# First expert layer: the bias of the normalisation moves from GpSimd to VectorE

## The chip, the core and the metric

The kernel runs on one core of a Trainium2 chip. The metric is the device time of one execution in microseconds, the median of three. The engines are named as the profile names them: PE (TensorE, matrix products), DVE (VectorE), ACT (ScalarE), POOL (GpSimd) and SP (the queue that issues most of the loads and stores). Each engine works through its own list of instructions in order, and a semaphore wait in that list holds everything behind it.

## What is computed

Two layers, each a recurrent or attention branch multiplied by the SiLU of a mixture of experts, over 8 sequences of 512 tokens of width 128. What matters here is in the first layer. Its branch is a state-space scan over 256 channels and 16 states, its experts are 24 two-layer experts in 4 groups with a layer norm and a ReLU between the two layers:

```
h = dA * h + dBx                       # the scan, per channel and state
h1 = moe_apply(xf, combine, dispatch, W1, b1)
h1 = (h1 - mean) / sqrt(var + eps) * lw + lb
h1 = relu(h1)
out = moe_apply(h1, combine, dispatch, W2, b2)
```

The change touches `* lw + lb`: `lw` and `lb` are the normalisation's weight and bias, one row of 512 for each of the four groups.

## The kernel before

The first layer's scan and its experts run beside each other in one block (`scan_stage`, with `Moe0Experts` as `beside`). The scan has 64 steps: for each of 8 sequences, 8 pairs of states. In a step DVE forms two products with the broadcast B row (L783) and two with the C row of the step before (L793), each 128x1024 with one operand in PSUM, and then makes two scans (L811), 128x1024 with both operands in SBUF. Some steps have more: at the step's place q within its sequence, q = 0 and 1 end with a small product (L748, L752), q = 1 has the gate (L772), and q = 3 and 6 end with the four operations of a softplus (L760 to L766). PE broadcasts the rows into three PSUM buffers (L653), sums the states (L684), and ACT makes the decays (L596).

The experts' work is laid between these steps by `side_by_side` (L469): each engine's scan generator yields at fixed places, and at each of them the experts' generator for that engine is advanced by one `yield`. So the order on an engine is written out at build time; nothing decides it at run time but the semaphores. DVE's scan generator yields twice in a step: behind the four products, and behind the two scans (and the softplus or small product that follows them).

From about step 22 the experts are in their combination. It goes over 16 units of two token tiles (128 tokens each). For one unit POOL gathers four blocks of first-layer outputs from DRAM (L1434), PE adds the gathered blocks and the experts' bias in PSUM (L1528, L1532), ACT copies the sum, takes mean and variance, refines the reciprocal root and centres the rows (L1643), POOL multiplies by `ln_w` and adds `ln_b` (L1454, L1456, each 128x1024, all operands in SBUF), ACT applies the ReLU (L1636), and SP stores the rows.

POOL's list has, for each unit u, the four gathers of unit u+1 and then the two arithmetic instructions of unit u-3 (`weigh`). These two wait for a window of the scan: `wait_window(FIRST_WINDOW + n)` with `FIRST_WINDOW = 26` lets unit n's arithmetic start when the scans of step 25+n are done, or, where that step ends with a softplus, when the softplus is done. Unit n's ReLU on ACT waits for the semaphore `weighted`, which the addition raises. The rows live in a ring of six tiles (`self.ro`), so that three units are under way.

DVE has no part in the combination before the change: `Moe0Experts.vector` sets two constants and ends.

Of the kernel before, what the change touches and what calls it, by code (L numbers as in the profile page):

```python
# [20 lines left out]
ALU = mybir.AluOpType  # L21
# [15 lines left out]
HG, E0, C0, HID = 4, 24, 86, 512  # L37
# [11 lines left out]
class Chain:  # L49


    def __init__(self, eng, sem):
        self.eng, self.sem, self.n = eng, sem, 0
# [425 lines left out]
PE_SLOTS, ACT_SLOTS, DVE_SLOTS = 4, 2, 2  # L479
# [826 lines left out]
class Moe0Experts:  # L1306
# [13 lines left out]
    def __init__(self, nc, ctx, w, r, arena, xn_dram, W1, y1_rows, r_dram, W2, y2_rows, gathered,  # L1320
                 w1_in):
        self.nc, self.w, self.r = nc, w, r
        self.xn_rows = xn_dram.rearrange("p t d -> (p t) d")
        self.y1_rows = y1_rows
        self.y1_dram = y1_rows[0:NO_ROW, :].rearrange("(h e c) n -> h e c n", h=HG, e=E0)
        self.r_dram, self.r_rows = r_dram, r_dram.rearrange("p t n -> (p t) n")
        self.W1, self.W2 = W1, W2
        self.y2_dram = y2_rows[0:NO_ROW, :].rearrange("(h e c) n -> h e c n", h=HG, e=E0)
        s = Scope(nc, ctx, "e")


        weights = Arena(arena[:, 0:3 * HID])
        self.w1 = weights.sb("w1", [P, 3, HID])
        self.w2 = self.w1.rearrange("p r (f d) -> p r f d", f=FC)
        first, middle, second = (Arena(arena[:, 3 * HID:]) for _ in range(3))
        self.xg = first.sb("xg", [CP, 4, HG, XW])
        self.xgT = first.sb("xgT", [P, 2, HG * CP])
        self.out1 = first.sb("out1", [CP, 2, HG, HID])
        self.yk = middle.sb("yk", [P, 4, 2, HID])
        self.hb = middle.sb("hb", [P, 4, HID])  # L1340
        self.ro = middle.sb("ro", [P, 6, HID])
        self.rg = second.sb("rg", [CP, 3, HG, HID])
        self.rT = second.sb("rT", [P, 3, FC * CP])
        self.out2 = second.sb("out2", [CP, 2, HG, D])
        self.stats = s.sb("stats", [P, NT, 3])
        self.total = s.sb("total", [P, NT])
        self.square = s.sb("square", [P, NT])
        self.rstd = s.sb("rstd", [P, NT])
        self.nm = s.sb("nm", [P, NT])
        self.squares = s.sb("squares", [P, HID])  # L1350
        self.eps = s.sb("eps", [P, 2])
        self.eps_set = s.sem("eps_set")
        self.newton = s.sem("newton")
        self.log_ready = s.sem("log_ready")
        self.bank = s.ps("bank", [P, 2, 512])
        self.scanned = self.u_ready = None
        self.chain = s.sem("chain")
        self.mean_ready = s.sem("mean_ready")
        self.piece_made = s.sem("piece_made")
        self.piece_read = s.sem("piece_read")  # L1360
        self.biased = s.sem("biased")
        self.combined = s.sem("combined")
        self.var_ready = s.sem("var_ready")
        self.scale_ready = s.sem("scale_ready")
        self.centred = s.sem("centred")
        self.p_chain = s.sem("p_chain")
        self.weighted = s.sem("weighted")
        self.r_ready = s.sem("r_ready")
        self.turned2 = s.sem("turned2")
        self.rT_ready = s.sem("rT_ready")  # L1370
        self.product2 = s.sem("product2")
        self.out2_ready = s.sem("out2_ready")
        self.w1_in = w1_in
        self.gathered1, self.gathered_y, self.gathered2 = gathered[0:4], gathered[4:8], gathered[8:11]
        self.stored1 = [s.sem(f"stored1{i}") for i in range(2)]
        self.stored_r = [s.sem(f"stored_r{i}") for i in range(3)]
        self.w2_in = [s.sem(f"w2_in{i}") for i in range(3)]
        self.stored2 = [s.sem(f"stored2{i}") for i in range(2)]
# [36 lines left out]
    def pool(self, pool):  # L1415
        nc, r = self.nc, self.r

        def gather_x(e):
            if e >= E0:
                return  # L1420
            if e >= 4:
                pool.wait_ge(self.piece_read, 5 * (e - 3))
            for h in range(HG):
                nc.gpsimd.indirect_dma_start(  # L1424
                    out=self.xg[:, e % 4, h, :], out_offset=None, in_=self.xn_rows,
                    in_offset=bass.IndirectOffsetOnAxis(ap=r.tab[:, h, e:e + 1], axis=0),
                ).then_inc(self.gathered1[e % 4], 16)

        def gather_y(u):
            for t in range(2 * u, min(2 * u + 2, NT)):  # L1430
                if t >= 4:
                    pool.wait_ge(self.biased, t - 3)
                for k in range(2):
                    nc.gpsimd.indirect_dma_start(  # L1434
                        out=self.yk[:, t % 4, k, :], out_offset=None, in_=self.y1_rows,
                        in_offset=bass.IndirectOffsetOnAxis(ap=r.back[:, k, t:t + 1], axis=0),
                    ).then_inc(self.gathered_y[t % 4], 16)

        def wait_window(i):

            b, q = divmod(i - 1, DS // 2)
            if q in (3, 6):
                pool.wait_ge(self.u_ready, 2 * (b + 1) + (q - 3) // 3 + 1)
            else:
                pool.wait_ge(self.scanned, 2 * i)

        def weigh(u):

            pool.wait_ge(self.centred, 2 * u + 2)
            wait_window(FIRST_WINDOW + u)  # L1450
            t = 2 * u
            ro = self.ro[:, t % 6:t % 6 + 2, :]
            g = slice(t % HG, t % HG + 2)
            nc.gpsimd.tensor_tensor(ro, ro, self.w["ln_w"][:, g, :], ALU.mult).then_inc(self.p_chain, 1)  # L1454
            pool.wait_ge(self.p_chain, u + 1)
            nc.gpsimd.tensor_tensor(ro, ro, self.w["ln_b"][:, g, :], ALU.add).then_inc(self.weighted, 1)  # L1456

        def gather_r(e):
            if e >= E0:
                return  # L1460
            if e >= 3:
                pool.wait_ge(self.turned2, HG * (e - 2))
            for h in range(HG):
                nc.gpsimd.indirect_dma_start(  # L1464
                    out=self.rg[:, e % 3, h, :], out_offset=None, in_=self.r_rows,
                    in_offset=bass.IndirectOffsetOnAxis(ap=r.tab[:, h, e:e + 1], axis=0),
                ).then_inc(self.gathered2[e % 3], 16)

        for e in range(E0):
            gather_x(e + self.AHEAD)  # L1470
            yield
        for i in range(2):
            pool.wait_ge(self.stored1[i], 16 * (E0 // 2))
        gather_y(0)
        yield
        for u in range(self.UNITS + 4):
            gather_y(u + 1)
            if 3 <= u < self.UNITS + 3:
                weigh(u - 3)
            yield  # L1480
        for i in range(3):
            pool.wait_ge(self.stored_r[i], 16 * len(range(i, self.UNITS, 3)))
        for e in range(self.AHEAD):
            gather_r(e)
        yield
        for e in range(E0):
            gather_r(e + self.AHEAD)
            yield
# [202 lines left out]
    def vector(self, dve):  # L1691
        nc, r, v = self.nc, self.r, self.nc.vector
        link = Chain(dve, self.chain)
        link(v.memset(self.eps[:, 0:1], 1e-6))
        v.memset(self.eps[:, 1:2], 1.5).then_inc(self.eps_set, 1)
        yield


class Moe0Output:
# [117 lines left out]
    def link(self, dve, ins):  # L1817
        self.linked += 1
        ins.then_inc(self.d_chain, 1)
        dve.wait_ge(self.d_chain, self.linked)  # L1820
# [1197 lines left out]
```

## Time and profile before

| | us |
|---|---|
| median of 3 runs | 1442.43 (1440.59 to 1442.75) |
| the profiled execution: its own time | 1438.98 |
| the profiled execution: its span | 1436.1 |
| DVE busy in the span | 1199.1 (83%) |
| PE busy in the span | 1258.3 (88%) |
| ACT busy in the span | 883.8 (62%) |
| POOL busy in the span | 681.2 (47%) |

The span runs from the first to the last instruction recorded; the execution's own time is 2.9 us longer. The shares are averages over stages that are limited by different engines, so the stretch in which the change lies is read by itself. That stretch is steps 26 to 40 of the scan, from 371.55 to 551.63 us of the span: from the end of step 25's scans, behind which POOL's first multiplication starts, to the start of step 41's products.

### The profile page before, as it was taken

The numbers are of one execution on the slowest core, as the hardware profiler recorded it, in microseconds if no ns is written. First come the engines' busy times: TensorE is split into PE (matmuls) and PEld (weight loads), VectorE is DVE, ScalarE is ACT, GpSimd is POOL, SyncE is SP. The second block draws the span as 40 slices with busy tenths as digits, with TensorE's granted clock in tenths as the row PEclk, the third lists the DMA queues.
The fourth block names the chain that finished last, engine by engine and source line by source line (L and its number), as shares of the span: only waits on it lengthen the run. The fifth ranks groups of instructions, "written<-read, shape, count | busy, mean of one in ns | idle before, by whom it ended". The sixth has DMA issues, their size and how long they took to land. (4 is left out here: it accounts for less than half of the span.)

```text
span 1436.1 us, 21390 instructions
## 1 busy us (share of the span) xinstructions
PE 1258.3 (88%) x7254; PEld 874.3 (61%) x7260; DVE 1199.1 (83%) x2410; ACT 883.8 (62%) x2114; POOL 681.2 (47%) x633
## 2 busy tenths in 40 slices
PE   6988798887988865999897997799999999999997
PEld 5444354443443433888896775467667777777775
DVE  6868999998888889999996778688898755568876
ACT  5577667575988885556553657756456444544462
POOL 0026565615688855655651775338640143146300
PEclk9999999999889977999998899899999999999999
DMA  8014555455233422445552721010002044213200
GB/s 257 1 24 114 144 144 155 130 142 150 90 107 128 133 74 84 136 138 142 163 146 61 235 53 37 15 42 4 1 2 59 7 111 127 62 33 49 28 29 31
DMA packets 86021, 128.82 MB, mean 90 GB/s; under 512 B 15488, under 2 KB 50657, under 8 KB 85306
## 3 DMA queue, kind: packets, MB, share of 16 engines
q1 hardware_dynamic: 66458, 75.70, 18.0%
q0 software_dynamic: 19456, 51.77, 14.0%
q8 instruction: 58, 0.95, 0.3%
q14 instruction: 49, 0.40, 0.1%
HBM read 86.66 MB, written 40.77 MB: 89 GB/s over the span
## 5 line engine op out<-in xcount | busy, mean ns | idle before, releaser
L811 DVE TENSOR_TENSOR_SCAN sc_st<-sc_dA,sc_st 128x1024 f32<-128x1024 f32 x128 | 291.0, 2317 | 0.0
L2359 DVE COPY at_pT<-at_p_t 128x512 f32<-128x512 f32 (+1 forms) x192 | 108.8, 599 | 105.2 <-PE at_p_t L2136 105.0
L793 DVE TENSOR_TENSOR sc_st<-sc_st,sc_p_bc 128x1024 f32<-128x1024 f32 x128 | 155.7, 1217 | 31.6 <-PE sc_p_bc L653 31.5
L596 ACT ACTIVATE sc_dA<-sc_dt,g_state 128x511 f32<-128x511 f32 x256 | 168.8, 709 | 6.2 <-DVE sc_st L811 5.5
L783 DVE TENSOR_TENSOR sc_st<-sc_u,sc_p_bc 128x1024 f32<-128x1024 f32 x128 | 155.1, 1212 | 7.5 <-PE sc_p_y L684 6.5
L1464 POOL DMA_INDIRECT g_state<-r_scratch,moe_tab x96 | 122.2, 1273 | 82.0 <-PE e_bank L1560 55.2
L1424 POOL DMA_INDIRECT g_state<-xn_scratch,moe_tab x88 | 117.5, 1335 | 84.3 <-ACT g_state L1584 48.1
L2232 ACT ACTIVATE at_pr<-at_pr,at_nmx 128x512 f32<-128x512 f32 (+3 forms) x256 | 140.2, 552 | 23.3 <-DVE at_nmx L2318 23.2
L2116 PE MATMUL at_p_s<-g_xT,at_qT 128*128 128x512 f32 (+3 forms) x512 | 149.4, 435 | 0.0
L653 PE MATMUL sc_p_bc<-sc_bc,mamba_sel 96*128 96x512 bf16 x256 | 102.4, 401 | 51.3 <-DVE sc_st L783 47.4
L684 PEld LDWEIGHTS sc_p_y<-g_ident,sc_st 128*128 128x128 f32 x1024 | 121.7, 144 | 27.5 <-issue 14.1
L684 PE MATMUL sc_p_y<-g_ident,sc_st 128*128 128x128 f32 x1024 | 136.1, 277 | 2.0 <-DVE sc_st L793 1.9
L1434 POOL DMA_INDIRECT g_state<-y_scratch,moe_back x64 | 93.1, 1455 | 56.8 <-DMA y_scratch<-g_state 32.3
L2318 DVE CUSTOM_DVE_ANT_0 at_pr<-at_p_s,l_mask_wide 128x512 f32<-128x512 f32 (+3 forms) x256 | 110.4, 486 | 6.0 <-PE at_p_s L2116 5.5
L2116 PEld LDWEIGHTS at_p_s<-g_xT,at_qT 128*128 128x128 f32 x512 | 83.0, 191 | 50.2 <-issue 32.1
L1513 PE MATMUL e_bank<-g_state 128*96 128x512 f32 x192 | 99.0, 614 | 10.7 <-ACT g_state L1574 10.6
L1547 PE MATMUL e_bank<-g_state 128*96 128x128 f32 x768 | 101.7, 276 | 4.4 <-ACT g_state L1675 4.0
L1584 ACT ACTIVATE g_state<-e_bank,g_state 96x512 f32<-96x512 f32 x96 | 65.0, 680 | 62.1 <-PE e_bank L1513 60.3
L2136 PEld LDWEIGHTS at_p_t<-g_ident,at_pr 128*128 128x128 f32 x640 | 74.8, 141 | 43.0 <-DVE at_pT L2359 31.5
L2136 PE MATMUL at_p_t<-g_ident,at_pr 128*128 128x128 f32 x640 | 91.6, 274 | 6.9 <-DVE at_pT L2359 6.0
L1684 ACT ACTIVATE g_state<-e_bank 128x384 f32<-128x384 f32 x96 | 46.8, 487 | 77.7 <-PE e_bank L1560 77.6
L2570 POOL DMA_INDIRECT f_m<-y_scratch,l_back x64 | 60.4, 943 | 71.7 <-DMA y_scratch<-f_out 33.4
(343 smaller groups left out, 2718.9 us busy)
## 6 DMA issues: line engine op xcount, KB each, us to landing
y_scratch<-g_state SPq DMA_DIRECT2D x24, 768.0 KB, 5.2
g_state<-W SPq DMA_DIRECT2D x48, 256.0 KB, 5.5
r_scratch<-g_state SPq DMA_DIRECT2D x16, 512.0 KB, 2.6
y_scratch<-g_state SPq DMA_DIRECT2D x24, 192.0 KB, 2.7
xn_scratch<-g_state SPq DMA_DIRECT2D x16, 256.0 KB, 4.2
g_state<-x SPq DMA_DIRECT2D x4, 512.0 KB, 7.0
g_state<-xn_scratch SPq DMA_DIRECT2D x8, 256.0 KB, 5.8
g_state<-x SPq DMA_DIRECT2D x1, 2048.0 KB
```

What stands on the lines that cost most here:

```text
L596: ins = nc.scalar.activation(dA[:, m % 4, j, 1:L], dt[:, b % 2, h, 1:L], ACT.Exp, scale=negA[:, h, 2 * q + j:2 * q + j + 1])
L684: ins = nc.tensor.matmul(p_y[:, t, h * P:(h + 1) * P], st[:, m + h, j, t * P:(t + 1) * P], w["ident"], is_transpose=True, start=False, sto ...
L783: nc.vector.tensor_tensor(st[:, m % RS:m % RS + 2, j, :], u[:, b % 2, :, :], p_bc[:, k % 3, :].unsqueeze(1).broadcast_to([P, HALF, L]), AL ...
L793: nc.vector.tensor_tensor(states, states, p_bc[:, k % 3, :].unsqueeze(1).broadcast_to([P, HALF, L]), ALU.mult).then_inc(row_used, 1)
L811: nc.vector.tensor_tensor_scan(st[:, m % RS, :, :].rearrange("p a b -> p (a b)"), dA[:, m % 4, :, :].rearrange("p a b -> p (a b)"), st[:, ...
L1424: nc.gpsimd.indirect_dma_start(out=self.xg[:, e % 4, h, :], out_offset=None, in_=self.xn_rows, in_offset=bass.IndirectOffsetOnAxis(ap=r.ta ...
L1464: nc.gpsimd.indirect_dma_start(out=self.rg[:, e % 3, h, :], out_offset=None, in_=self.r_rows, in_offset=bass.IndirectOffsetOnAxis(ap=r.tab ...
L2116: ins = nc.tensor.matmul(p_s[:, bank, c:c + K], qT[:, n % 3, i * P:(i + 1) * P], xaT[:, b, 0:K], start=True, stop=True)
L2136: ins = nc.tensor.transpose(p_t[:, bank, c + (i - j) * P:c + (i - j + 1) * P], pr[:, n % 3, sbank, sc + j * P:sc + (j + 1) * P], w["ident"])
L2232: ins = nc.scalar.activation(row, row, ACT.Exp, scale=-1.0, bias=nmx[:, n % 2, i:i + 1], accum_out=sums[:, n % 4, i:i + 1])
L2318: ins = v.tensor_tensor_reduce(out=pr[:, n % 3, bank, c:c + K], in0=p_s[:, bank, c:c + K], in1=w["mask_wide"][:, L - K:L], scale=1.0, scal ...
L2359: v.tensor_copy(pT[:, n % 2, part, 0:cols], p_t[:, PT_BANK[part], 0:cols]).then_inc(pT_ready, 1)
```

## The change

The addition of `ln_b` is taken from POOL and given to DVE. POOL's `weigh` keeps its two waits (for the centred rows and for the window of the scan) and its multiplication, which now raises a new semaphore, `multiplied`; the wait between multiplication and addition on POOL goes. `Moe0Experts.vector` gets a loop: it passes 50 yields (two for each of `E0 + 1` units), and then, in unit n's turn, waits for `multiplied` and adds `ln_b`, which raises `weighted`.

```
-        self.p_chain = s.sem("p_chain")
+        self.multiplied = s.sem("multiplied")
...
-            nc.gpsimd.tensor_tensor(ro, ro, self.w["ln_w"][:, g, :], ALU.mult).then_inc(self.p_chain, 1)
-            pool.wait_ge(self.p_chain, u + 1)
-            nc.gpsimd.tensor_tensor(ro, ro, self.w["ln_b"][:, g, :], ALU.add).then_inc(self.weighted, 1)
+            nc.gpsimd.tensor_tensor(ro, ro, self.w["ln_w"][:, g, :], ALU.mult).then_inc(self.multiplied, 1)
...
-        yield
+        yield from [None] * (DVE_SLOTS * (E0 + 1))
+        for u in range(self.UNITS + 4):
+            yield
+            if 3 <= u < self.UNITS + 3:
+                n = u - 3
+                ro = self.ro[:, 2 * n % 6:2 * n % 6 + 2, :]
+                dve.wait_ge(self.multiplied, n + 1)
+                v.tensor_tensor(ro, ro, self.w["ln_b"][:, 2 * n % HG:2 * n % HG + 2, :],
+                                ALU.add).then_inc(self.weighted, 1)
+            yield
```

On DVE, the list at the end of step 25 and in step 26 stands as follows before the change. `sc_st` are the states, `sc_p_bc` a broadcast row in PSUM; L811 are the scans.

```order
L811 SCALAR_TENSOR_TENSOR sc_st<-sc_dA,sc_st 128x1024 [waits sc_decay_ready,sc_row_used]
L811 SCALAR_TENSOR_TENSOR sc_st<-sc_dA,sc_st 128x1024 [waits sc_decay_ready]
L752 TENSOR_TENSOR sc_bc<-sc_logs 32x512 [waits sc_mid_copied]
L783 TENSOR_TENSOR sc_st<-sc_u,sc_p_bc 128x2x512 [waits sc_hc_used,sc_row_ready,sc_bc_done]
L793 TENSOR_TENSOR sc_st<-sc_st,sc_p_bc 128x2x512 [waits sc_scanned,sc_row_ready]
```

After it, the same place and on to the next addition. `g_state` is the ring of rows, `moe_ln_b` the bias.

```order
L811 SCALAR_TENSOR_TENSOR sc_st<-sc_dA,sc_st 128x1024 [waits sc_decay_ready,sc_row_used]
L811 SCALAR_TENSOR_TENSOR sc_st<-sc_dA,sc_st 128x1024 [waits sc_decay_ready]
L752 TENSOR_TENSOR sc_bc<-sc_logs 32x512 [waits sc_mid_copied]
L1701 TENSOR_TENSOR g_state<-g_state,moe_ln_b 128x1024 [waits e_multiplied,sc_bc_done]
L783 TENSOR_TENSOR sc_st<-sc_u,sc_p_bc 128x2x512 [waits sc_hc_used,sc_row_ready]
L793 TENSOR_TENSOR sc_st<-sc_st,sc_p_bc 128x2x512 [waits sc_scanned,sc_row_ready]
L783 TENSOR_TENSOR sc_st<-sc_u,sc_p_bc 128x2x512 [waits sc_row_ready]
L793 TENSOR_TENSOR sc_st<-sc_st,sc_p_bc 128x2x512 [waits sc_scanned,sc_row_ready]
L811 SCALAR_TENSOR_TENSOR sc_st<-sc_dA,sc_st 128x1024 [waits sc_decay_ready,sc_row_used]
L811 SCALAR_TENSOR_TENSOR sc_st<-sc_dA,sc_st 128x1024 [waits sc_decay_ready]
L1701 TENSOR_TENSOR g_state<-g_state,moe_ln_b 128x1024 [waits e_multiplied]
```

Sixteen additions (L1701) stand each between a step's scans and the next step's products, in steps 25 to 40.

On POOL, the difference at the first two units. L1434 are the gathers, L1454 the multiplications.

```order
 L1454 TENSOR_TENSOR g_state<-g_state,moe_ln_w 128x1024 [waits sc_scanned,e_centred]
-L1456 TENSOR_TENSOR g_state<-g_state,moe_ln_b 128x1024 [waits e_p_chain]
-L1434 DMA g_state<-y_scratch,moe_back 128x512 [waits e_biased]
-L1434 DMA g_state<-y_scratch,moe_back 128x512
-L1434 DMA g_state<-y_scratch,moe_back 128x512 [waits e_biased]
-L1434 DMA g_state<-y_scratch,moe_back 128x512
-L1454 TENSOR_TENSOR g_state<-g_state,moe_ln_w 128x1024 [waits sc_scanned,e_centred]
-L1456 TENSOR_TENSOR g_state<-g_state,moe_ln_b 128x1024 [waits e_p_chain]
```

The sixteen additions go from this list; gathers and multiplications keep their order, and each multiplication keeps its wait for `sc_scanned` (or `sc_u_ready`).

## Rows read from the trace of the kernel before

**Rows 1.** The page's head, its span and instructions.

```profile
span 1436.1 us, 21390 instructions
```

**Rows 2.** Busy time by stretch; columns named in the head line.

```profile
core 0: us, PE busy (x) PEld busy (x) DVE busy (x) ACT busy (x) POOL busy (x), PEclk, DMA share, GB/s
371.55:551.63 180.08, 140.99 (x491) 68.33 (x490) 153.74 (x112) 152.79 (x405) 142.63 (x75) 0.86 0.34 108
551.63:776.00 224.37, 203.51 (x1687) 181.63 (x1687) 221.99 (x162) 130.11 (x238) 126.54 (x98) 0.96 0.48 132
```

**Rows 3.** Waits of DVE, 371.55 to 551.63: total us, times, longest.

```profile
DVE sc_st L793 <- PE sc_p_bc L653: 21.6, 7, 4.3
DVE sc_st L783 <- PE sc_p_y L684: 4.2, 4, 1.5
```

**Rows 4.** Timeline of POOL, one unit: start, duration, what, idle before.

```profile
448.17 2.36 POOL L1454 TENSOR_TENSOR g_state<-g_state,moe_ln_w 128x1024 f32<-128x1024 f32 x1
450.61 2.35 POOL L1456 TENSOR_TENSOR g_state<-g_state,moe_ln_b 128x1024 f32<-128x1024 f32 x1
453.10 2.91 POOL L1434 DMA_INDIRECT g_state<-y_scratch,moe_back  x1
456.31 1.85 POOL L1434 DMA_INDIRECT g_state<-y_scratch,moe_back  x1 [0.30 <-issue]
...
459.71 0.95 POOL L1434 DMA_INDIRECT g_state<-y_scratch,moe_back  x1 [0.30 <-issue]
460.68 2.37 POOL L1454 TENSOR_TENSOR g_state<-g_state,moe_ln_w 128x1024 f32<-128x1024 f32 x1
```

**Rows 5.** Timeline of DVE, pairs of scans and the products behind them.

```profile
403.20 4.47 DVE L811 TENSOR_TENSOR_SCAN sc_st<-sc_dA,sc_st 128x1024 f32<-128x1024 f32 x2
407.58 1.20 DVE L783 TENSOR_TENSOR sc_st<-sc_u,sc_p_bc 128x1024 f32<-128x1024 f32 x1
408.70 1.22 DVE L793 TENSOR_TENSOR sc_st<-sc_st,sc_p_bc 128x1024 f32<-128x1024 f32 x1
...
412.09 6.58 DVE L811 TENSOR_TENSOR_SCAN sc_st<-sc_dA,sc_st 128x1024 f32<-128x1024 f32 x2
...
476.49 5.73 DVE L811 TENSOR_TENSOR_SCAN sc_st<-sc_dA,sc_st 128x1024 f32<-128x1024 f32 x2
...
502.13 4.84 DVE L811 TENSOR_TENSOR_SCAN sc_st<-sc_dA,sc_st 128x1024 f32<-128x1024 f32 x2
```

**Rows 6.** Timeline of all engines: POOL started by DVE's scans.

```profile
515.54 4.47 DVE L811 TENSOR_TENSOR_SCAN sc_st<-sc_dA,sc_st 128x1024 f32<-128x1024 f32 x2
...
520.15 2.35 POOL L1454 TENSOR_TENSOR g_state<-g_state,moe_ln_w 128x1024 f32<-128x1024 f32 x1 [5.11 <-DVE sc_st L811]
```

**Rows 7.** Timeline of all engines: ACT started by POOL's addition.

```profile
500.27 2.37 POOL L1456 TENSOR_TENSOR g_state<-g_state,moe_ln_b 128x1024 f32<-128x1024 f32 x1
...
502.67 1.06 ACT L1636 ACTIVATE g_state<-g_state 128x1024 f32<-128x1024 f32 x1 [2.27 <-POOL g_state L1456]
```

**Rows 8.** Timeline of all engines: step 25's small product, POOL's first multiplication.

```profile
371.67 0.68 DVE L752 TENSOR_TENSOR sc_bc<-sc_logs 32x512 bf16<-32x512 f32 x1
371.80 2.79 POOL L1454 TENSOR_TENSOR g_state<-g_state,moe_ln_w 128x1024 f32<-128x1024 f32 x1 [10.01 <-DVE sc_st L811]
```

**Rows 9.** Timeline of DVE: a half-width product, both operands in SBUF.

```profile
396.48 0.69 DVE L766 TENSOR_TENSOR sc_u<-sc_dt,g_xT 128x512 f32<-128x512 f32 x1
```

**Rows 10.** Timeline of PE: one step's work, and one block's products earlier.

```profile
392.40 3.78 PE L1532 MATMUL e_bank<-g_state,g_ident 128*128 128x512 f32 x4
...
398.71 1.12 PE L1528 MATMUL e_bank<-moe_b_experts,moe_GT 24*128 24x512 f32 x2
399.76 1.98 PE L1532 MATMUL e_bank<-g_state,g_ident 128*128 128x512 f32 x4
...
407.26 1.12 PE L1528 MATMUL e_bank<-moe_b_experts,moe_GT 24*128 24x512 f32 x2
```

**Rows 11.** Busy time in 2 us stretches; columns as in Rows 2.

```profile
528.00:530.00 2.00, 0.00 (x0) 0.00 (x0) 2.00 (x2) 1.94 (x7) 0.00 (x0) 0.89 0.35 139
530.00:532.00 2.00, 0.00 (x0) 0.00 (x0) 1.90 (x4) 1.90 (x8) 0.00 (x0) 0.50 0.00 0
```

## The prediction

> **What bounds the kernel now.** I read the page's head first for the span [rows 1], then the busy time by stretch, because the change lies in one stage only. In the 180.08 us from the end of step 25's scans to the start of step 41's products DVE is busy for 153.74 us, more than any other engine; from there to the end of the scan it is busy for 221.99 of 224.37 us [rows 2]. DVE therefore sets the pace of the scan, and behind the changed stretch it has no slack in which a delay could vanish: what the stretch gains or loses reaches the end of the kernel at its full size.
>
> The next view is DVE's waits in that stretch. It stands idle for 180.08 - 153.74 = 26.3 us [rows 2], and 21.6 + 4.2 = 25.8 us of them are waits for PE: for a broadcast row and for the states' sums [rows 3]. PE is late because the combination's work stands between its rows, and what feeds that work is POOL. The timeline of POOL shows a unit that has no idle time but the gaps of issue: multiplication, addition and four gathers fill the 460.68 - 448.17 = 12.5 us from one multiplication to the next [rows 4]. A DVE step without waits is shorter than that (below), so for most of the stretch POOL's cycle sets the pace, and DVE's waits are where it shows.
>
> A second loss is hidden in DVE's busy time. A pair of scans lasts 4.47 us when nothing disturbs it; where POOL's arithmetic reaches into it, it lasts 6.58, 5.73 or 4.84 us [rows 5]. In the stretch there is one pair of the first kind, one of the second, and four between 4.82 and 4.84. Together they are 2.1 + 1.3 + 4 x 0.36 = 4.8 us too long.
>
> So DVE's own work in the stretch is 153.7 - 4.8 = 148.9 us, and 26.3 + 4.8 = 31.1 us are lost to POOL's length. That is the most that the change can give back.
>
> **The change part by part.** *What leaves POOL.* Sixteen additions of 2.35 us, with the gap ahead of the next gather 453.10 - 450.61 = 2.49 us each [rows 4]. POOL's unit falls from 12.5 to 10.0 us. If DVE then needs longer than this for a step, POOL is no longer the pace, and its arithmetic no longer reaches into a scan, since only the multiplication is left and DVE waits for its end. I take all 31.1 us as given back; the other end is none of it (0 us), which is a rival below.
>
> *What DVE gets.* The order shows each addition directly behind the scans of the same step whose end opens POOL's window: POOL's multiplication waits for `scanned` of step 25+n, and DVE's next instruction after those scans waits for that multiplication. This is the step that I think decides. The multiplication, which up to now lay beside DVE's products of the next step, has nothing beside it on DVE any more: behind the waiting addition all four products and the scans of the next step are queued, and PE (for its row buffers) and ACT (for its decay buffers) wait for those. For each unit, then:
>
> - From the scans' end to the multiplication's start. DVE issues the next instruction 407.58 - 403.20 = 4.38 us after a pair of scans starts [rows 5]. A pair starts at 515.54, so it ends in this sense at 519.92, and the waiting POOL starts at 520.15 [rows 6]: 0.23 us.
> - The multiplication: 2.35 us [rows 6].
> - From POOL's end to the waiting engine's start. No row shows POOL releasing DVE. The nearest is POOL releasing ACT: 500.27 + 2.37 = 502.64, and ACT starts at 502.67 [rows 7]: 0.03 us.
> - The addition. The trace has no addition of this size with both operands in SBUF on DVE. From below it is bounded by a product of half the width with both operands in SBUF, 0.69 us [rows 9], from above by a scan of the full width, 4.38 / 2 = 2.19 us [rows 5]. Nearest is the 128x1024 product with one operand in PSUM: 1.20 to 1.22 us long, 408.70 - 407.58 = 1.12 to 1.13 us to the next start [rows 5]. I take 1.13.
>
> That is 0.23 + 2.35 + 0.03 + 1.13 = 3.74 us a unit, and 59.8 us for 16. In four of the sixteen steps (q = 0 and 1) a small product stands between scans and addition. It was paid already, and now lies beside the multiplication; in step 25 it takes 0.68 us and the multiplication beside it 2.79 us in place of 2.35 [rows 8]. I take back 0.5 us for each: 2.0 us. In steps with a softplus POOL waits for the softplus' end, so the same 3.74 us come behind it.
>
> *The sum.* 148.9 + 59.8 - 2.0 = 206.7 us in place of 180.1: 26.6 us longer. A step is then 206.7 / 16 = 12.9 us, against POOL's 10.0 us of work, so the assumption that POOL is no longer the pace holds with 2.9 us to spare. The profiled execution took 1438.98 us and would take 1465.6, its span 1436.1 [rows 1] would be 1462.7. The median of the runs before, 1442.43, is 3.5 us over the profiled one; with the same difference the new median is 1469.0 us.
>
> *What costs nothing.* ACT's ReLU now waits for DVE in place of POOL. Relative to the scans' end the rows are ready after 3.7 us, against some 5.0 us before (0.23 and two instructions), so the store and the later gathers are no later relative to the scan. ACT is busy 152.79 us of the stretch [rows 2], less than the 206.7 us that it will have. The new instructions on DVE issue no transfer, and SP's queue is unchanged.
>
> *A rule weighed against a row.* POOL's gathers take 2.91 and 1.85 us in the part of the unit that lies beside DVE's scans, and 0.95 us elsewhere [rows 4]; an addition on DVE that also reads two operands in SBUF could therefore hold the first gather behind each multiplication by its own 1.13 us. POOL's unit would be 11.1 us, still below 12.9. The Trainium skill's page "SBUF — State Buffer", section "Who interferes with whom", holds the opposite for such a `tensor_tensor`: it is said to take only the shared read port, while writing descriptors needs the write port. This case's scans, also with two SBUF inputs, do lengthen the gathers, so I go by the row; by the page POOL would have 1.1 us more to spare, and the sum is the same.
>
> **The rivals.** *PE falls to its lower clock and becomes the pace (slower still).* At the full clock PE's work in a step with two tiles takes 407.26 - 398.71 = 8.55 us; the same four products take 1.98 us there and 3.78 us earlier [rows 10], so at the lower level a step is 8.55 x 3.78 / 1.98 = 16.3 us. With 12.9 us a step PE would idle over 4 us in each, and a stretch without matmuls is what comes ahead of a fall in this trace: none run from 528 to 532 us, and the granted clock goes from 0.89 to 0.50 [rows 11], the 1.2 GHz level. PE decides once more than (12.9 - 8.55) / (16.3 - 8.55) = 56% of its work in a step is done at that level. If that is so in half of the sixteen steps, 8 x (16.3 - 12.9) = 27 us come on top: 1496 us. The Trainium skill's page "TensorE: Matmul & The Clock Gate", section "HAM oscillation — how this bites in real kernels", speaks for this: a loop that makes TensorE wait in each round can keep sending its clock down. Against it: with DVE waiting a row is wanted later, and the stretch's granted clock was 0.86 in the mean with about the same density of work [rows 2].
>
> *POOL stays late.* If all four gathers took 2.91 us with 0.3 us between them, POOL's unit would be 12.9 + 2.4 = 15.3 us, above 12.9, and DVE would wait for it: 16 x 2.4 = 38 us more, 1507 us. It decides above 12.9 us. Against it: only two of four gathers are long in a unit that now has two instructions on POOL beside the scan [rows 4].
>
> *The multiplication is ready when DVE comes to the addition (faster).* Then DVE pays 16 x 1.13 = 18.1 us and gets back the 31.1: 148.9 + 18.1 = 167.0 us, 13.1 us less, 1429.3 us. For this the multiplication would have to start at least 2.4 us before the step's scans end, that is, the order would have to give DVE the addition a step later or POOL its window a step earlier. Both waits in the order stand as they do, so for this I would have had to misread which step's scans raise the semaphore; between the two ends it would come out even if DVE's wait were 0.8 us a unit in place of 2.6.
>
> **How the numbers follow.** The forecast has 82%, PE's clock 10%, a late POOL 3%, the ready multiplication and what lies between it and the forecast 5%. A difference of about 0.2% is what a measurement of this kernel can tell from no change, 2.9 us here. From the cases: faster 0.04, the same 0.01, slower 0.95. The likeliest time is 1469 us. The addition's bounds move it by 16 x (0.61 - 1.13) = -8 us (the half-width product less its 0.08 us of overlap) and by 16 x (2.19 - 1.13) = +17 us: 1461 to 1486. With a part of the PE case the range for 8 in 10 is 1460 to 1490.
>
> **What would show it.** Right: in the profile after, DVE's largest wait in this stretch is L1701 for POOL's L1454, 16 times about 2.6 us (some 40 us in all); the waits for L653 and L684 nearly vanish; no pair of scans there is longer than 4.5 us; POOL's multiplications all start 0.2 us behind a scan or softplus, with idle time before them; the stretch lasts about 207 us and the one behind it 224 as now. A DVE wait for L1454 of well under 1 us would prove the forecast wrong in its main step; waits for L653 beside it that stay above 10 us would mean that POOL or PE still sets the pace, and the time would be above 1480.

## The result and the profile after

The changed kernel takes 1468.01 us in the median of four runs (1467.57 to 1471.54), against 1442.59 for the kernel before (1440.59 to 1445.08): 25.4 us slower, a ratio of 1.0182 with a 95% interval of 1.0155 to 1.0209. The forecast was 1469 us.

The busy time by stretch comes first, as in [rows 2]. The changed stretch, again from the end of step 25's scans to the start of step 41's products, now runs from 374.05 to 580.86 us. The columns are those of [rows 2].

```profile
374.05:580.86 206.81, 148.73 (x491) 72.34 (x490) 167.52 (x129) 154.93 (x407) 91.38 (x60) 0.82 0.29 94
580.86:805.23 224.37, 203.10 (x1687) 181.53 (x1687) 222.11 (x162) 128.96 (x236) 120.08 (x96) 0.96 0.48 132
```

The stretch lasts 206.81 us in place of 180.08, 26.7 us more, and the one behind it lasts 224.37 us in both kernels. DVE is busy 13.8 us longer, POOL 51.3 us less, and DVE's idle time has grown from 26.3 to 39.3 us. (The two profiled spans, 1465.8 and 1436.1, differ by 29.7 us. Of these 2.5 us are there before the stretch begins, where the two programs are alike, and belong to the two executions, not to the change.)

What DVE waits for in that stretch, as in [rows 3], is one line:

```profile
DVE g_state L1701 <- POOL g_state L1454: 38.8, 16, 2.5
```

Sixteen additions, sixteen waits, 38.8 us. Both waits for PE of [rows 3] are gone. One unit in the timeline of DVE reads (start, duration, what, idle time before):

```profile
382.82 4.47 DVE L811 TENSOR_TENSOR_SCAN sc_st<-sc_dA,sc_st 128x1024 f32<-128x1024 f32 x2
389.82 1.23 DVE L1701 TENSOR_TENSOR g_state<-g_state,moe_ln_b 128x1024 f32<-128x1024 f32 x1 [2.53 <-POOL g_state L1454]
390.96 1.21 DVE L783 TENSOR_TENSOR sc_st<-sc_u,sc_p_bc 128x1024 f32<-128x1024 f32 x1
```

and the same time on POOL:

```profile
387.44 2.35 POOL L1454 TENSOR_TENSOR g_state<-g_state,moe_ln_w 128x1024 f32<-128x1024 f32 x1 [4.45 <-DVE sc_st L811]
389.93 1.97 POOL L1434 DMA_INDIRECT g_state<-y_scratch,moe_back  x1
392.21 0.95 POOL L1434 DMA_INDIRECT g_state<-y_scratch,moe_back  x1 [0.30 <-issue]
393.46 0.95 POOL L1434 DMA_INDIRECT g_state<-y_scratch,moe_back  x1 [0.30 <-issue]
394.71 0.94 POOL L1434 DMA_INDIRECT g_state<-y_scratch,moe_back  x1 [0.30 <-issue]
402.86 2.35 POOL L1454 TENSOR_TENSOR g_state<-g_state,moe_ln_w 128x1024 f32<-128x1024 f32 x1 [7.21 <-DVE sc_u L766]
```

The two engines hand one piece of work to and fro. The scans end at 382.82 + 4.38 = 387.20, POOL starts at 387.44, ends at 389.79, DVE starts at 389.82 and is free for the next step at 390.96. (The 2.53 us in the row are counted from the recorded end of the scans, 382.82 + 4.47 = 387.29.) POOL, which in [rows 4] had no idle time, now stands idle for 4.45 and 7.21 us ahead of its multiplications. All its waits of this kind in the stretch are:

```profile
POOL g_state L1454 <- DVE sc_st L811: 77.6, 12, 10.3
POOL g_state L1454 <- DVE sc_u L766: 34.7, 4, 13.1
```

### The profile page after: what moved, and what is told of

It reads as the page before. It is cut to its first block and busy times, and to the rows that moved or that the text cites. A ratio compares the mean times of both kernels' runs of the same rounds, so it can differ in the third digit from the quotient of the medians.

```text
span 1465.8 us, 21398 instructions
## 1 busy us (share of the span) xinstructions
PE 1268.6 (87%) x7260; PEld 880.2 (60%) x7260; DVE 1212.8 (83%) x2426; ACT 885.2 (60%) x2114; POOL 622.1 (42%) x617
## 5 line engine op out<-in xcount | busy, mean ns | idle before, releaser
L811 DVE TENSOR_TENSOR_SCAN sc_st<-sc_dA,sc_st 128x1024 f32<-128x1024 f32 x128 | 286.1, 2278 | 0.0
L653 PE MATMUL sc_p_bc<-sc_bc,mamba_sel 96*128 96x512 bf16 x256 | 104.1, 408 | 95.0 <-DVE sc_st L783 91.3
L596 ACT ACTIVATE sc_dA<-sc_dt,g_state 128x511 f32<-128x511 f32 x256 | 169.0, 710 | 13.8 <-DVE sc_st L811 12.9
L793 DVE TENSOR_TENSOR sc_st<-sc_st,sc_p_bc 128x1024 f32<-128x1024 f32 x128 | 155.7, 1217 | 8.6 <-PE sc_p_bc L653 8.5
L684 PEld LDWEIGHTS sc_p_y<-g_ident,sc_st 128*128 128x128 f32 x1024 | 125.5, 147 | 29.1 <-issue 15.6
L684 PE MATMUL sc_p_y<-g_ident,sc_st 128*128 128x128 f32 x1024 | 139.7, 281 | 1.2 <-DVE sc_st L793 1.2
L653 PEld LDWEIGHTS sc_p_bc<-sc_bc,mamba_sel 96*128 96x128 bf16 x256 | 25.9, 101 | 139.0 <-DVE sc_st L783 117.6
L1434 POOL DMA_INDIRECT g_state<-y_scratch,moe_back x64 | 77.9, 1217 | 55.4 <-DMA y_scratch<-g_state 32.4
L2143 PEld LDWEIGHTS at_p_t<-g_ident,at_pr 128*128 128x128 f32 x640 | 74.9, 141 | 42.8 <-DVE at_pT L2366 31.1
```

Source lines behind the costliest of these rows:

```text
L596: ins = nc.scalar.activation(dA[:, m % 4, j, 1:L], dt[:, b % 2, h, 1:L], ACT.Exp, scale=negA[:, h, 2 * q + j:2 * q + j + 1])
L653: nc.tensor.matmul(p_bc[:, k % 3, :], w["sel"][:, n * P:(n + 1) * P], bc3[:, b % 2, :], start=True, stop=True).then_inc(row_ready, 1)
L684: ins = nc.tensor.matmul(p_y[:, t, h * P:(h + 1) * P], st[:, m + h, j, t * P:(t + 1) * P], w["ident"], is_transpose=True, start=False, sto ...
L793: nc.vector.tensor_tensor(states, states, p_bc[:, k % 3, :].unsqueeze(1).broadcast_to([P, HALF, L]), ALU.mult).then_inc(row_used, 1)
L811: nc.vector.tensor_tensor_scan(st[:, m % RS, :, :].rearrange("p a b -> p (a b)"), dA[:, m % 4, :, :].rearrange("p a b -> p (a b)"), st[:, ...
L2143: ins = nc.tensor.transpose(p_t[:, bank, c + (i - j) * P:c + (i - j + 1) * P], pr[:, n % 3, sbank, sc + j * P:sc + (j + 1) * P], w["ident"])
```

## The experiments

All are timed against the kernel before on the same chip, in three rounds; that kernel's median was 1444.2, 1441.1 and 1441.2 us in the three groups (e1 to e4, e5 to e8, e9 and e10). To compare stretches I use the time from step 25's small product (L752) to that of step 41, the sixteen steps 26 to 41: 561.77 - 371.67 = 190.1 us before the change, 591.01 - 374.17 = 216.8 after it. (The stretch of [rows 2] ends with step 40 and so has fifteen steps.)

**e3: the wait without the addition's length.** The small addition leaves out the bias of all other columns.

```
-                v.tensor_tensor(ro, ro, self.w["ln_b"][:, 2 * n % HG:2 * n % HG + 2, :],
+                v.tensor_tensor(ro[:, :, 0:1], ro[:, :, 0:1], self.w["ln_b"][:, 2 * n % HG:2 * n % HG + 2, 0:1],
                                 ALU.add).then_inc(self.weighted, 1)
```

> The addition stays where the change puts it, with its wait, but adds only the first column of each tile (128x2 elements); the rest of the bias is left out. Theory: the wait of 2.3 to 2.6 us stays 16 times and only the addition's 1.13 us goes, less some 0.1 us for the small one: 16 us less than the changed kernel, about 1452 us, still 9 us over the kernel before. Rival (the addition is the price): the loss goes with it, 1442 us or less.

1453.06 us (1451.1 to 1456.6), ratio 1.0066 (1.0043 to 1.009). The wait is unchanged, to the tenth of a microsecond:

```profile
DVE g_state L1701 <- POOL g_state L1454: 38.8, 16, 2.5
```

The sixteen steps take 200.4 us, 16.4 less than in the changed kernel. So the addition's length is 16 us of the loss, and with the wait alone the kernel is still slower than before.

**e4: no bias at all.** POOL's multiplication raises `weighted`, and DVE's loop is taken out.

```
-            nc.gpsimd.tensor_tensor(ro, ro, self.w["ln_w"][:, g, :], ALU.mult).then_inc(self.multiplied, 1)
+            nc.gpsimd.tensor_tensor(ro, ro, self.w["ln_w"][:, g, :], ALU.mult).then_inc(self.weighted, 1)
```

> The bias is left out; POOL's multiplication raises the ReLU's semaphore and DVE has nothing to do in the combination. This measures what POOL's cycle costs the kernel before. Theory by DVE's count: all 31.1 us come back, the stretch is 148.9 us, about 1411 us. Rival: with a step of 9.3 us ACT (152.8 us busy in the stretch before) or PE sets the pace, and only half or so comes back: stretch 155 to 170 us, 1418 to 1433 us.

1421.32 us (1419.91 to 1422.89), ratio 0.9849 (0.9815 to 0.9882): 22.9 us faster, which is in the range of the rival. The sixteen steps take 170.0 us; without any loss they would take 190.1 - 31.1 = 159.0. Of the remaining 11 us, 10.6 are DVE's waits for PE:

```profile
DVE sc_st L783 <- PE sc_p_y L684: 5.3, 3, 3.5
DVE sc_st L793 <- PE sc_p_bc L653: 5.3, 3, 2.7
```

A step of DVE's own work is 159.0 / 16 = 9.9 us (the expectation's 9.3 divides fifteen steps by sixteen), and at that pace PE becomes the next limit. In the changed kernel the longer step hid that, and all 31.1 us came back.

**e1: the addition a step later, behind the scans.** The unit's number is the only edit, so that the addition of unit n follows the scans of step 26+n.

```
-            if 3 <= u < self.UNITS + 3:
-                n = u - 3
+            if 4 <= u:
+                n = u - 4
```

> The addition of unit n stands behind the scans of step 26+n in place of 25+n; POOL's window is as it was. Theory (the loss is the exposed multiplication): DVE finds the multiplication done, its waits for it go from 38.8 us to under 3 us, a unit costs DVE 1.14 us in place of 3.74, and the stretch of steps 26 to 41 comes to some 148.9 + 18 = 167 us: about 1429 us, faster than both kernels. The addition now starts as POOL's next multiplication does, so that multiplication lengthens from 2.35 to some 3 us without a cost. Rival (the addition itself is the price, since DVE and POOL hold each other up): the time stays above 1455 us. A second rival: ACT's ReLU, a whole step later, makes ACT late for PE's tiles, and part of the waits for PE come back: about 1440 us.

1520.19 us (1516.23 to 1521.92), ratio 1.0537 (1.0502 to 1.0572): 76 us slower than before. The time lies in the range of the first rival (above 1455 us), but not for its reason: DVE does not wait for POOL any more, but for PE. That is what the second rival expected, at some 1440 us:

```profile
DVE sc_st L793 <- PE sc_p_bc L653: 76.5, 11, 7.6
DVE sc_st L783 <- PE sc_p_y L684: 7.0, 5, 2.4
```

The timeline of all engines shows one turn of that wait:

```profile
381.85 1.20 DVE L1701 TENSOR_TENSOR g_state<-g_state,moe_ln_b 128x1024 f32<-128x1024 f32 x1
...
383.08 1.06 ACT L1634 ACTIVATE g_state<-g_state 128x1024 f32<-128x1024 f32 x1 [7.99 <-DVE g_state L1701]
...
387.06 0.57 ACT L1653 ACTIVATE g_state<-e_bank 128x512 f32<-128x512 f32 x1
...
387.77 2.07 PE L1526 MATMUL e_bank<-moe_b_experts,moe_GT 24*128 24x512 f32 x2 [7.03 <-ACT g_state L1653]
...
389.77 3.78 PE L1530 MATMUL e_bank<-g_state,g_ident 128*128 128x512 f32 x4
...
393.35 0.53 PE L653 MATMUL sc_p_bc<-sc_bc,mamba_sel 96*128 96x512 bf16 x1
...
393.92 1.22 DVE L793 TENSOR_TENSOR sc_st<-sc_st,sc_p_bc 128x1024 f32<-128x1024 f32 x1 [7.47 <-PE sc_p_bc L653]
```

ACT's ReLU waits for the addition, and ACT's list has the reading of PE's tile (L1653) behind it. PE's next tile waits for that reading, PE's row (L653) is queued behind the tile, and DVE's product (L793) waits for the row. The four products of 3.78 us show the clock at its lower level as well; the granted clock in these sixteen steps was 0.73 in the mean. So an addition that is too late for ACT costs more than one that is too early for POOL.

**e2: the addition a step later, behind the products.** The same edit, with the addition ahead of the turn's first `yield`, so 4.4 us earlier.

> The addition of unit n stands behind the four products of step 26+n, ahead of its scans. Theory: the multiplication ends some 2.6 us after the scans of step 25+n and the products take 4.5 us, so DVE does not wait for it; stretch about 167 us, 1429 us. The rows are ready 4.8 us earlier for ACT than behind the next scans, so if ACT's turn matters, this one is the faster of the two by up to 10 us; if only DVE's count matters, both agree within 2 us. Rival (the addition itself is the price): above 1455 us.

1441.74 us (1439.64 to 1446.8), ratio 0.9995 (0.9975 to 1.0015): the exposed multiplication is gone, so the price is not the addition itself, but 12 us of what was expected are missing, and the time is that of the kernel before. The waits of ACT and DVE in the sixteen steps:

```profile
ACT g_state L1634 <- DVE g_state L1700: 30.0, 13, 5.5
```

```profile
DVE sc_st L793 <- PE sc_p_bc L653: 13.5, 7, 3.2
DVE sc_st L783 <- PE sc_p_y L684: 0.3, 1, 0.3
```

**e5: as e2, with ACT's ReLU later on its list.** The waits of e1 and e2 suggest a loop through the ReLU; here the ReLU stands between the reads of the two tiles.

```
-            if 4 <= u:
+            def relu():
                 n = u - 4
                 act.wait_ge(self.weighted, n + 1)
                 rows = ro[:, 2 * n % 6:2 * n % 6 + 2, :]
                 nc.scalar.activation(rows, rows, ACT.Relu).then_inc(self.r_ready, 1)
...
                                         accum_out=self.square[:, t:t + 1]).then_inc(self.var_ready, 1)
+                    if t == 2 * u and 4 <= u:
+                        relu()
...
+            if u >= self.UNITS:
+                relu()
             yield
```

> The addition behind the next step's products (as in e2), and ACT's ReLU moved on its list from ahead of the centring to between the two tiles' reads of the same turn, some 3 us later. Theory (in e1 and e2 the loss is a loop: DVE's addition, ACT's ReLU, ACT's read of the tile's bank behind it, PE's next tile, PE's row behind that, DVE's product): ACT no longer waits for the addition, the 30 us of that wait in e2 go below 5, DVE's 15 us of waits for L653 fall, and the time comes to 1431 to 1438 us. Rival (with an addition on DVE the stage is full whatever the order): the same as e2, 1440 to 1444 us.

1427.53 us (1426.13 to 1431.54), ratio 0.9903 (0.9873 to 0.9933), which is 13.5 us faster than the kernel before, and a little beyond the range expected. In the sixteen steps DVE has no wait that the view lists, and ACT's has shrunk:

```profile
ACT g_state L1634 <- DVE g_state L1705: 8.1, 3, 4.2
```

They take 552.62 - 375.81 = 176.8 us; DVE's own work with the sixteen additions is 159.0 + 18.1 = 177.1. DVE is busy for 176.2 of the 176.8 us: it is the stage at DVE's limit.

**e6: no ReLU of its own.** As e2, but the ReLU's lines go from ACT's list, SP stores the sum, and ACT's copy in the second layer applies the ReLU.

```
-            sp.wait_ge(self.r_ready, u + 1)
+            sp.wait_ge(self.weighted, u + 1)
...
-                nc.scalar.activation(self.rT[:, n % 3, :], bank[:, 0, 0:FC * CP], ACT.Copy).then_inc(self.rT_ready, 1)
+                nc.scalar.activation(self.rT[:, n % 3, :], bank[:, 0, 0:FC * CP], ACT.Relu).then_inc(self.rT_ready, 1)
```

> The addition behind the next step's products, and no ReLU of its own: SP stores the rows as the addition leaves them, and ACT's copy of the transposed rows in the second expert layer (L1682 there) applies the ReLU in place of a copy, which gives the same values. Theory: the loop through ACT is cut altogether and ACT has 1.05 us less in a unit; DVE's waits for PE under 8 us, 1427 to 1434 us, faster than both kernels. Rival: PE at its lower clock keeps DVE waiting, 1438 us or more.

1427.73 us (1426.36 to 1433.07), ratio 0.9898 (0.9862 to 0.9933): the same as e5. The rest of ACT's work has room enough, so taking the ReLU away brings nothing beyond moving it.

**e7: the kernel before, with e6's edit of the ReLU alone.**

> The kernel before with only the ReLU moved into the second layer's copy; POOL still multiplies and adds. Theory (POOL's 12.5 us a unit are the pace before): ACT's waits for POOL vanish, but the pace does not change: within 4 us of the kernel before. Rival (the loop through ACT's ReLU, not POOL, is what held the kernel before): 15 us or more faster.

1443.79 us (1439.66 to 1450.03), ratio 1.0027 (1.0004 to 1.005). Cutting the loop through ACT gives nothing while POOL has both instructions: its length was the limit before.

**e8: e1 with e6's edit.**

> e1 with the ReLU moved into the second layer's copy: the addition still stands behind the next step's scans, 5 us later than in e6. Theory: e1's 76 us of loss were the loop through ACT's ReLU and go with it: 1430 to 1445 us; what may stay is ACT waiting for the store of the rows before it writes their buffer again. Rival (an addition at that place delays DVE by itself): above 1490 us.

1434.4 us (1432.56 to 1436.75), ratio 0.9952 (0.9933 to 0.997). The same addition at the same place as in e1, and some 83 us less, each taken against the kernel before of its own group: e1's loss was the loop through the ReLU. Some 7 us over e5 and e6 remain. In the sixteen steps ACT waits 18.7 us for the stores of the rows, as was thought possible, but that is not where most of the 7 us lie: the sixteen steps take 178.0 us, against 176.8 in e5, and the eight steps behind them 83.9 against 80.6. Why those are longer is open.

**e9: the changed kernel with POOL's window one step earlier.** One number:

```
-EVEN_FROM, EVEN_TO, FIRST_WINDOW = 22, 43, 26
+EVEN_FROM, EVEN_TO, FIRST_WINDOW = 22, 43, 25
```

> The changed kernel with one number altered: FIRST_WINDOW 25 in place of 26, so POOL multiplies unit n behind the scans of step 24+n, and VectorE's addition stays where the change puts it, behind the scans of step 25+n. Theory (the loss is that the multiplication is let go only by the scans behind which the addition waits): the waits for L1454 go from 38.8 us to under 3, DVE pays the addition alone, and the time is 1428 to 1436 us. Rival (the place behind the scans is what costs, whatever POOL's window): above 1455 us. The multiplication now starts beside the addition of the unit before and may last some 3 us.

1431.51 us (1429.72 to 1433.69), ratio 0.9934 (0.9911 to 0.9956). The addition stands where the change puts it, and DVE goes through it without a wait:

```profile
382.64 4.46 DVE L811 TENSOR_TENSOR_SCAN sc_st<-sc_dA,sc_st 128x1024 f32<-128x1024 f32 x2
387.02 1.20 DVE L1701 TENSOR_TENSOR g_state<-g_state,moe_ln_b 128x1024 f32<-128x1024 f32 x1
388.14 1.21 DVE L783 TENSOR_TENSOR sc_st<-sc_u,sc_p_bc 128x1024 f32<-128x1024 f32 x1
```

All that is left of DVE's waits in the sixteen steps is one line, without L1454:

```profile
DVE sc_st L783 <- PE sc_p_y L684: 0.3, 1, 0.3
```

The sixteen steps take 553.27 - 376.25 = 177.0 us, 39.8 less than in the changed kernel. This is the shortest proof of the main step: some 35 us of the changed kernel's time (25.4 above the kernel before in one group, 9.7 below it in the other) hang on which step's scans open POOL's window.

**e10: e9 with e6's edit.**

> e9 with the ReLU moved into the second layer's copy, as in e6. If ACT's ReLU has no part in it, since in e9 the rows are ready when the next step begins, it agrees with e9 within 4 us; if the loop through ACT's ReLU still holds DVE in e9, it is faster by 5 us or more, at 1427 to 1431 us.

1430.27 us (1427.06 to 1432.2), ratio 0.9918 (0.9889 to 0.9947): within 4 us of e9. There the rows are ready for ACT at the start of the next step, early enough. e5, e6, e9 and e10 all beat both kernels; their intervals overlap, and which is best is open.

## Why the prediction was right

*DVE sets the pace and the loss passes through.* The stretch behind the changed one lasts 224.37 us in both kernels.

*The multiplication is exposed.* This was the step on which the forecast hung. It is shown from two sides: the wait is there sixteen times (38.8 us, forecast 16 x 2.6 less some 2 us), and it vanishes, with some 35 us, when POOL's window opens a step earlier (e9).

*The price of a unit.* From the scans' end to the next step: 0.24 us to POOL's start, 2.35 of multiplication, 0.03 back to DVE, 1.14 of addition, 3.76 in all against 3.74 forecast. The handover from POOL to DVE, taken from a row on ACT [rows 7], and the addition, taken from a product with one operand in PSUM [rows 5], were both right to 0.01 us. e3 gives the addition's part by itself: 16.4 us for sixteen, less the small additions. The small products give back less than the 2.0 us forecast: DVE's wait is 2.31 us behind the two at q = 1 and 1.94 behind the two at q = 0, in place of 2.53, so 1.6 us in all.

*What POOL gives back.* 31.1 us were taken as regained in full. In the changed kernel they were: no wait for PE and no lengthened scan is left (the longest single scan of the whole run is 2.30 us). The stretch without the units' price is 206.8 - 16 x 3.76 + 1.6 = 148.2 us, against 148.9 forecast. In the kernel that gives POOL the same relief without DVE's longer step (e4) only 22.9 us are regained, since PE then holds DVE up. The estimate was right in size because the step had become long, as the prediction's sum required, and would have been too large by itself.

*The rivals.* PE's clock did fall, from 0.86 to 0.82 in the stretch, but PE never held DVE up: it waits for DVE, as this line of the stretch shows.

```profile
PE sc_p_bc L653 <- DVE sc_st L783: 52.2, 14, 10.5
```

POOL was not late: from the multiplication's start to the last gather's end the unit shown above takes 394.71 + 0.94 - 387.44 = 8.2 us, less than the 10.0 to 11.1 forecast, since three of its four gathers now take 0.94 or 0.95 us.

The case on the faster side, that the multiplication is ready when DVE comes, was priced at 1429.3 us; made real it gives 1431.5 us (e9), or 1427.5 with the ReLU out of the way (e5). What that price left out is the loop through ACT: whoever moves the addition later and leaves the ReLU where it is gets 1441.7 (e2) or 1520.2 us (e1).

*A slip that did not reach the sum.* The prediction divides the stretch by sixteen, the number of the additions, but it holds fifteen steps. A step is 206.7 / 15 = 13.8 us and not 12.9. That gives POOL 3.8 us to spare in place of 2.9, and PE would decide only with (13.8 - 8.55) / (16.3 - 8.55) = 68% of its work at the lower clock in place of 56%. Both rivals were thus farther off than they were priced. The sum counts additions, not steps, and stands.

The measured difference of the medians, 25.4 us, is 1.2 us under the forecast 26.6, and the stretch by itself, 26.7 us, is 0.1 over it; the rest lies outside the stretch and within what executions differ by. That the stretch agrees to 0.1 us is partly luck: the units' price came out 0.3 us higher, the small products' share 0.4 us smaller and DVE's own work 0.7 us less than forecast, and these cancel.

## What to carry to other kernels

When work is split between two engines, look up what the first half waits for: if it is released by the instruction just ahead of the second half, the second engine pays for both halves in full, however little the second half is. Move the release or the second half by one step, and then follow the result's reader too, since an engine that waits in order for a late result holds up everything queued behind the wait. The price of such a wait can be summed from single rows; what its removal brings has to be checked for the next limit.

## What the runs showed of the hardware

An addition on DVE with both operands in SBUF does lengthen a gather that POOL issues beside it. In the changed kernel eleven multiplications have a gather behind them; it lies beside the addition and takes 1.94 to 2.03 us, while the next three of the unit shown above take 0.94 or 0.95. In e3, where the addition at the same place has 128x2 elements and takes 0.16 us, that first gather takes 0.98 us in all eleven units, so it is the addition that lengthens it, and not its place behind a multiplication:

```profile
391.77 0.98 POOL L1434 DMA_INDIRECT g_state<-y_scratch,moe_back  x1
```

The page "SBUF — State Buffer" of the Trainium skill, section "Who interferes with whom", infers that a `tensor_tensor` does not stand in the way of writing descriptors. The rows show that such a gather is held all the same. They do not show by what, since this gather also reads its row numbers (`moe_back`) from SBUF. It cost nothing, since POOL had idle time.

A multiplication on POOL that runs beside such an addition is lengthened too: the median is 2.35 us in the changed kernel, where the two never overlap, and 3.19 us in e1, where they overlap in fifteen of the sixteen units. That agrees with the same section's rule, that a VectorE instruction with two SBUF inputs contends with a GpSimd instruction that reads SBUF.

```profile
L1454 POOL TENSOR_TENSOR g_state<-g_state,moe_ln_w x16: 2338/2347/2778, 374.3 to 577.3; 128x1024 f32<-128x1024 f32 x16
```

```profile
L1454 POOL TENSOR_TENSOR g_state<-g_state,moe_ln_w x16: 2551/3192/3786, 372.3 to 623.1; 128x1024 f32<-128x1024 f32 x16
```

The first line is the changed kernel's, the second e1's; the columns behind the count are the shortest, the median and the longest duration in ns.

It can also be the addition that is lengthened. In one unit of e1 POOL's recorded start lies 0.60 us ahead of the addition's; the multiplication takes 2.79 us there, as beside a small product alone, and the addition 3.27 us in place of the usual 1.20:

```profile
511.04 3.27 DVE L1701 TENSOR_TENSOR g_state<-g_state,moe_ln_b 128x1024 f32<-128x1024 f32 x1
```

In two other units POOL's recorded start lies 0.35 and 0.36 us ahead, and there it is still the multiplication that is lengthened, to 3.78 and 3.79 us.
